# Output projection in rounded halves, two low parts on GpSimd, all orders set anew with nine streams

## The chip, the cores and the metric

One core of a Trainium2 chip runs the whole program in one launch. The metric is the device time of that launch in microseconds; every time here is of this one core. The engines are TensorE (PE in the rows, PEld for its weight loads), VectorE (DVE), ScalarE (ACT), GpSimd (POOL) and SyncE (SP), which issues the DMAs.

## The reference

`x` is 128 graphs of 128 nodes with 256 features, in float32. Four residual layers follow each other, each fed with `h = relu(layernorm(x))`:

```python
h = relu(layernorm(x)); x = x + L0(h)   # 8 heads of 32, masked by adj
#   qkv = h @ w_qkv; attn = softmax(where(adj == 0, -inf, q k^T * scale)); o = attn v
#   o = o @ w_proj + b_proj; L0 = o + layernorm(o) * gamma + beta
h = relu(layernorm(x)); x = x + L1(h)   # rel = adj^T * (h Wq^T)(h Wk^T)^T; rel / ||rel||; rel @ (h Wv^T)
h = relu(layernorm(x)); x = x + L2(h)   # hw = h W; e = leaky_relu(s1 + s2) * adj; elu(softmax(e) hw + beta hw)
h = relu(layernorm(x)); x = x + L3(h)   # (adj h) @ weight + bias
```

## The kernel before

The 128 graphs are 64 pairs, and one pair goes through the four layers in a software pipeline of `STREAMS = 8` stages. Step `t` of the unrolled loop works on eight pairs at once: stage `s` of it on pair `p_s = t - s`, if `on[s]`. Each engine has its own `step`, a list of blocks written out by hand in the order in which that engine is to take them; nothing else orders the work. An engine waits at a semaphore when a block needs what another engine makes (`wait_ge(..., done(p))`), when it would overwrite a single buffer that is still to be read (`wait_before`: the reader of the pair before must be through), or when a PSUM bank is still held by its last readers (`bank_free`). The eight PSUM banks (`mid[:, 0..3]` and `bank4..7`) are shared by some twenty uses, by a table of names at the top.

What the text below speaks of, in the order of the data:

- `z[k]` is the normalised input of layer `k`. PE transposes it (L329) into PSUM; ACT writes its relu, rounded to fp32r, as `h_t[k][0]` (the high part, L581, L589 and L644), and DVE writes the rest, relu minus high part, as `h_t[k][1]` (the low part, `relu_lo`, L730). A product of two such pairs is three fp32r matmuls (`product`, L313: high by high, high by low, low by high).
- `h_t[0]` feeds three products: q and k in the step in which it is made (stage 0) and the values v0 in the next step (stage 1). It is a single buffer, so ACT may write the next pair's high part only when v0 of the pair before is through (`v0_psum`).
- `scores()` (L357) fills the four banks of `mid`; DVE masks them and takes the least value of each row (`least_masked(r)`, L715); ACT takes the exponentials of head group `r` (`exps(r)`, L541, four activations); PE transposes them (`transpose_probs(r)`, L348); ACT copies each bank to SBUF; PE multiplies by the values and by ones (`heads_times_values`, L369 and L373). Scores and heads run on small tiles of the array (32 rows or 32 columns), all else on the whole array.
- ACT makes the reciprocal of the sums (L655, L658), DVE the scaled heads `o_t` (L830), and PE the output projection in plain float32 (`rows_f32`, L320).
- Layer 1 multiplies `h_t[1]` by the folded `w_qk` (g, then `g_t` copied by ACT, L563) and by `w_v` (v1), layer 2 `h_t[2]` by `w_gat` (hw, with `e_sum` made by ACT from it, L638), layer 3 `y_t` by `w_out`.
- POOL takes the inverse square roots (L903, L905, L914) and four elementwise products or sums (L927, L934, L938, L942).

Of the kernel before, what the change touches and what calls it, by code (L numbers as in the profile page):

```python
# [6 lines left out]
def gnn_stack(nc, x, adj, adj_t, w_qkv, w_proj, b_proj, gamma, beta_ln, w_q, w_k, w_v_t,  # L7
# [21 lines left out]
    STREAMS = 8  # L29
# [5 lines left out]
    with ctx:  # L35
# [27 lines left out]
        w_qk_p = parts("w_qk", [128, C, D])  # L63
        w_gat_p = parts("w_gat", [128, C, DX])
# [50 lines left out]
        o_t = sb("o_t", [128, 2, C, N])  # L115
        o = sb("o", [128, 2, D])
# [33 lines left out]
        q_bank = bank6[:]  # L150
        k_bank = mid[:, 1]
        v_bank = bank6[:]
        p0_bank = bank5[:]
        p1_bank = mid[:, 3]
        p2_bank = bank4[:]
        p3_bank = bank7[:]
        heads_bank = bank5[:]
        sums_bank = bank7[:]
        o_bank = bank5[:]
        z1_bank = bank6[:]  # L160
        g_bank = bank4[:]
        v1_bank = bank7[:]
        rel_bank = mid[:, 3]
        rel_v_bank = mid[:, 2]
        z2_bank = mid[:, 2]
        hw0_bank = mid[:, 2]
        hw1_bank = mid[:, 1]
        s2_bank = mid[:, 0]
        att_bank = mid[:, 0]
        u_bank = mid[:, 0]  # L170
        y_t_bank = bank4[:]
        y_bank = bank7[:]
# [13 lines left out]
        y_lo_ready = sem("y_lo_ready")  # L186
        shift0_ready = sem("shift0_ready")
# [64 lines left out]
        SPLIT = [(w_v_sb[:], w_v_p)]  # L252
# [26 lines left out]
        def _(sp):  # L279
# [9 lines left out]
            def step(t, par, load, store):  # L289
                pb, p_out = t - 1, t - 7  # L290

                if load:
                    i = (par + 1) % 2
                    sp.wait_ge(z_ready[0], done(pb))
                    sp.wait_ge(xb_ready, done(pb))
                    sp.dma_start(x0[:, i], x_pairs[pb + 2]).then_inc(x_in[i], 16)
                if store:
                    i = (par + 7) % 2
                    sp.wait_ge(x4_ready, done(p_out))
                    sp.dma_start(out_pairs[p_out], x4[:, i]).then_inc(x_out[i], 16)  # L300

            for t in range(PAIRS + 7):
                step(t, t % 2, 1 <= t < PAIRS + 1 - 2, t >= 7)
# [4 lines left out]
        def _(pe):  # L308
# [91 lines left out]
            def step(t, par, on):  # L400
                p0, p1, p2, p3, p4, p5, p6, p7, p8 = [t - s for s in range(STREAMS + 1)]

                if on[1]:
                    pe.wait_ge(q_ready, done(p1))
                    pe.wait_ge(k_ready, done(p1))
                    bank_free(pe, (e_sum_ready, p5, 2), (x3_ready, p6, 1), (att_t_ready, p6, 1))
                    bank_free(pe, (k_ready, p1, 1), (hw_ready, p5, 2))
                    bank_free(pe, (x2_ready, p4, 2), (hw_ready, p5, 2), (h_lo_ready[2], p5, 1))
                    bank_free(pe, (probs_t_ready[1], p2, 1), (sum_sq_ready, p4, 1))
                    scores().then_inc(scores_psum, 1)  # L410
                    pe.wait_ge(h_lo_ready[0], done(p1))
                    bank_free(pe, (h1_full_ready, p3, 1), (q_ready, p1, 1), (h_lo_ready[0], p1, 1))
                    rows(halves(v_bank), h_t[0], w_qkv_p, 2 * D, D).then_inc(v0_psum, 1)
                if on[3]:
                    pe.wait_ge(h_lo_ready[1], done(p3))
                    bank_free(pe, (y_lo_ready, p7, 1), (probs_t_ready[2], p2, 1))
                    columns(g_bank, w_qk_p, 0, h_t[1]).then_inc(g_psum, 1)
                if on[7]:
                    pe.wait_ge(y_lo_ready, done(p7))
                    bank_free(pe, (ln_sum_ready, p2, 1), (probs_t_ready[3], p2, 1), (v1_ready, p4, 1))  # L420
                    rows(halves(y_bank), y_t_p, w_out_p, 0, D).then_inc(y_psum, 1)
                if on[2]:
                    pe.wait_ge(o_norm_ready, done(p2))
                    bank_free(pe, (o_norm_ready, p2, 1), (probs_t_ready[0], p2, 1))
                    rows_f32(halves(o_bank), lambda b, c: o_t[:, b, c], w_proj_sb).then_inc(o_psum, 1)
                if on[0]:
                    pe.wait_ge(z_ready[0], done(p0))
                    bank_free(pe, (v0_ready, p1, 1), (h1_full_ready, p3, 1), (q_ready, p1, 1))
                    transposes(z0_bank, z[0]).then_inc(h_t_psum[0], 1)
                if on[4]:  # L430
                    pe.wait_ge(z_ready[2], done(p4))
                    bank_free(pe, (max_ready[2], p1, 1), (x2_ready, p4, 2), (hw_ready, p5, 2))
                    transposes(z2_bank, z[2]).then_inc(h_t_psum[2], 1)
                if on[3]:
                    pe.wait_ge(g_ready, done(p3))
                    pe.wait_ge(h1_full_ready, done(p3))
                    bank_free(pe, (max_ready[3], p1, 1), (probs_t_ready[1], p2, 1))
# [5 lines left out]
                if on[5]:  # L443
                    pe.wait_ge(att_norm_ready, done(p5, 2))
                    bank_free(pe, (max_ready[0], p1, 1), (e_sum_ready, p5, 2), (x3_ready, p6, 1))
                    for b in range(2):
                        last = pe.transpose(att_bank[:, b * N:(b + 1) * N], att_norm[:, b], ident[:])
                    last.then_inc(att_t_psum, 1)
                if on[1]:
                    pe.wait_ge(probs_ready[2], done(p1))  # L450
                    bank_free(pe, (g_ready, p3, 1), (y_lo_ready, p7, 1))
                    transpose_probs(2).then_inc(probs_t_psum[2], 1)
                if on[3]:
                    pe.wait_ge(h_lo_ready[1], done(p3))
                    bank_free(pe, (x4_ready, p7, 1), (ln_sum_ready, p2, 1), (probs_t_ready[3], p2, 1))
                    rows(halves(v1_bank), h_t[1], w_v_p, 0, D).then_inc(v1_psum, 1)
                if on[5]:
                    pe.wait_ge(att_t_ready, done(p5))
                    bank_free(pe, (att_t_ready, p5, 1), (max_ready[0], p1, 1), (e_sum_ready, p5, 2))
                    for b in range(2):  # L460
                        last = pe.matmul(u_bank[:, b * D:(b + 1) * D], att_t[:, b], hw[:, b, 0:D], start=True, stop=True)  # L461
                    last.then_inc(u_psum, 1)
                if on[1]:
                    pe.wait_ge(probs_ready[0], done(p1))
                    bank_free(pe, (o_ready, p2, 1), (o_norm_ready, p2, 1))
                    transpose_probs(0).then_inc(probs_t_psum[0], 1)
                if on[3]:
                    pe.wait_ge(rel_sq_ready, done(p3))
                    for b in range(2):
                        last = pe.matmul(rel_bank[:, 256 + b:257 + b], rel_sq[:, b], ones[:, 0:1], start=True, stop=True)  # L470
                    last.then_inc(sum_sq_psum, 1)
                if on[4]:
                    pe.wait_ge(h_lo_ready[2], done(p4))
                    bank_free(pe, (h_lo_ready[2], p4, 1), (max_ready[2], p1, 1), (x2_ready, p4, 2))
# [511 lines left out]
```

## Time and profile before

| | |
|---|---|
| time, median of 3 runs | 1482.62 us (1481.49 to 1482.86) |
| profiled execution: time, span | 1483.83 us, 1482.0 us |
| PE busy, share of the span | 1448.4 us, 98% |
| DVE, ACT, POOL busy | 1296.7, 1169.9, 606.9 us |
| mean granted TensorE clock | 0.991 of full speed |

The profiled execution's time lies 1.8 us above its span and 1.2 us above the median. A share of the span is an average over a start, an even middle and an end, which are read apart.

### The profile page before, as it was taken

The page shows a single profiled execution, that of the slowest core. Times are in us where ns is not written, and L with a number is a line of the kernel's source. Part 1 is how long each engine was busy: PE and PEld are TensorE (multiplying, and loading weights), DVE is VectorE, ACT ScalarE, POOL GpSimd, SP SyncE. Part 2 cuts the span into 40 slices and gives each one's busy share as a digit, 9 for nine tenths or more (in the row PEclk, how much of TensorE's full clock was granted, in tenths as well). Part 3 has the DMA queues.
Part 4 walks back from the last instruction along what each step waited for, and adds up shares of the span by engine and source line. Part 5 has one row for each costly group of instructions (what it writes and reads, how often), then busy time and mean ns, then how long its engine had stood idle before and what let it go on. Part 6 is the DMA issues. An engine that isn't in the chain of part 4 may idle for free.

```text
span 1482.0 us, 47177 instructions
## 1 busy us (share of the span) xinstructions
PE 1448.4 (98%) x15880; PEld 1375.0 (93%) x15880; DVE 1296.7 (87%) x5774; ACT 1169.9 (79%) x2948; POOL 606.9 (41%) x977
## 2 busy tenths in 40 slices
PE   6999999999999999999999999999999999999996
PEld 5899999999999999999999999999999999999985
DVE  3889988998989889889889889889889889889884
ACT  4788878878878878878878888888888878878763
POOL 3244434434434434444444444444444344344342
PEclk9999999999999999999999999999999999999997
DMA  3000101101000001000000010010010010000000
GB/s 111 16 16 23 30 17 30 30 18 30 24 23 30 22 25 30 19 28 30 17 31 30 16 31 30 16 31 30 17 30 30 16 30 30 17 30 30 11 21 30
DMA packets 38111, 39.87 MB, mean 27 GB/s; under 512 B 2416, under 2 KB 37488, under 8 KB 37872
## 3 DMA queue, kind: packets, MB, share of 16 engines
q1 hardware_dynamic: 37872, 36.84, 8.4%
q8 instruction: 131, 2.15, 0.6%
q14 instruction: 108, 0.88, 0.2%
HBM read 20.05 MB, written 16.78 MB: 25 GB/s over the span
## 4 chain that ended last, share of the span: by engine, by line
PE 95%; DVE 3%; issue 1%; POOL 0%; DMA 0%; ACT 0%; SPq 0%; POOLq 0%; DVEq 0%; ACTq 0%
PE bank L313 31%; PE mid L313 12%; PE bank L320 7%; PE bank L348 5%; PE mid L357 5%; PE bank L369 4%; PE mid L440 4%; PE mid L461 4%; PE bank L493 4%; PE bank L329 4%; PE bank L373 4%; PE mid L512 4%; PE mid L348 2%; PE mid L329 2%; PE mid L470 1%
## 5 line engine op out<-in xcount | busy, mean ns | idle before, releaser
L541 ACT ACTIVATE probs<-masked,neg_max 128x128 f32<-128x128 f32 x1024 | 312.0, 391 | 0.2 <-DVE neg_max L715 0.2
L715 DVE CUSTOM_DVE_ANT_0 masked<-mid,mask 128x128 f32<-128x128 f32 x1024 | 230.9, 287 | 18.1 <-issue 12.3
L905 POOL TENSOR_TENSOR rstd<-var_eps,minus_half 128x2 f32<-128x2 f32 x320 | 222.0, 694 | 25.1
L934 POOL TENSOR_TENSOR x3b<-x_up,b_out_less 128x512 f32<-128x512 f32 x64 | 82.3, 1287 | 283.1 <-DVE x L854 283.1
L903 POOL TENSOR_TENSOR var_eps<-mean_var,eps 128x2 f32<-128x2 f32 x320 | 62.9, 197 | 291.4 <-DVE mean_var L709 291.2
L705 DVE BATCH_NORM_STATS2 stats<-x 128x6 f32<-128x256 f32 x384 | 142.8, 413 | 3.5 <-DMA x<-in_x 3.5
L320 PE MATMUL bank<-w_proj_sb,o_t 128*128 128x256 f32 x512 | 121.0, 379 | 0.1
L348 PE MATMUL bank<-ident,probs 128*128 128x128 f32 x768 | 115.5, 273 | 1.9 <-ACT probs L541 1.0
L798 DVE SCALAR_TENSOR_TENSOR x<-mid,inv_norm,x 128x256 f32<-128x256 f32 x128 | 56.0, 480 | 70.1 <-PE mid L512 70.1
L914 POOL TENSOR_TENSOR inv_norm<-sum_sq,minus_half 128x2 f32<-128x2 f32 x64 | 66.7, 1043 | 119.8 <-DVE sum_sq L773 119.8
L938 POOL TENSOR_TENSOR xb<-x,b_proj_beta 128x512 f32<-128x512 f32 x64 | 81.5, 1273 | 60.7 <-DVE o_res L862 60.7
L369 PE MATMUL bank<-probs_t,v 128*32 128x128 f32 x2048 | 104.4, 276 | 0.0
L373 PE MATMUL bank<-probs_t,ones 128*32 128x128 f32 x2048 | 102.8, 273 | 0.0
L320 PEld LDWEIGHTS bank<-w_proj_sb,o_t 128*128 128x128 f32 x512 | 92.4, 190 | 10.3 <-DVE o_t L830 0.3
L348 PEld LDWEIGHTS bank<-ident,probs 128*128 128x128 f32 x768 | 91.7, 141 | 8.7 <-ACT probs L541 2.6
L621 ACT ACTIVATE probs_t<-bank 128x512 f32<-128x512 f32 x64 | 38.3, 598 | 74.6 <-PE bank L348 74.6
L724 DVE TENSOR_SCALAR z<-x,mean_var,rstd 128x256 f32<-128x256 f32 x256 | 92.1, 402 | 5.5 <-POOL rstd L905 5.3
L730 DVE SCALAR_TENSOR_TENSOR h_t_lo<-bank,h_t_hi 128x512 fp32r<-128x512 f32 x128 | 87.3, 682 | 4.8 <-ACT h_t_hi L589 4.3
L709 DVE BATCH_NORM_AGGREGATE mean_var<-stats 128x2 f32<-128x6 f32 x640 | 77.7, 163 | 13.8
L715 DVE DVE_READ_ACCUMULATOR2_ANT neg_max<- 128x1 f32 x1024 | 85.8, 84 | 0.0
L329 PE MATMUL bank<-ident,z 128*128 128x128 f32 x512 | 77.0, 273 | 2.9 <-issue 2.0
L313 PE MATMUL mid<-w_gat_hi,h_t_hi 128*128 128x258 f32 x256 | 79.0, 309 | 0.0
(142 smaller groups left out, 5373.4 us busy)
## 6 DMA issues: line engine op xcount, KB each, us to landing
x<-in_x SPq DMA_DIRECT2D x64, 256.0 KB, 2.9
out_x<-x SPq DMA_DIRECT2D x64, 256.0 KB, 3.2
w_qkv_sb<-in_w_qkv SPq DMA_DIRECT2D x1, 768.0 KB, 4.9
w_q_sb<-in_w_q SPq DMA_DIRECT2D x1, 256.0 KB, 4.8
w_k_sb<-in_w_k SPq DMA_DIRECT2D x1, 256.0 KB, 5.0
w_v_sb<-in_w_v_t SPq DMA_DIRECT2D x1, 256.0 KB, 5.7
w_proj_sb<-in_w_proj SPq DMA_DIRECT2D x1, 256.0 KB, 5.9
w_gat_x<-in_w_gat SPq DMA_DIRECT2D x1, 256.0 KB, 6.4
```

Of the source, the lines that this page charges most:

```text
L313: last = pe.matmul(dst, pick_l(lhs_t[a], c), pick_r(rhs[b], c), start=n == 0, stop=n == len(terms) - 1)
L320: last = pe.matmul(dsts[b], lhs_t(b, c), w[:, c], start=c == 0, stop=c == C - 1)
L329: last = pe.transpose(dst[:, (c * 2 + b) * N:(c * 2 + b + 1) * N], src[:, b, c * 128:(c + 1) * 128], ident[:])
L348: last = pe.transpose(dst[:, s * N:(s + 1) * N], probs[:, r, s], ident[:])
L369: pe.matmul(heads_bank[at, to], v0[:, b, hc * RG + r], probs_t[:, r, s], start=True, stop=True, tile_position=(0, r * HD))
L373: last = pe.matmul(sums_bank[at, to], ones[:], probs_t[:, r, s], start=True, stop=True, tile_position=(0, r * HD))
L541: last = act.activation(probs[:, r, s], masked[:, r, s], ACT.Exp, scale=-1.0, bias=neg_max[:, r, s:s + 1])
L705: dve.bn_stats(stats[:, k, b], src[:, b]).then_inc(ln_stats[k], 1)
L715: last = dve.tensor_tensor_reduce(out=masked[:, r, s], in0=mid[:, r, s * N:(s + 1) * N], in1=mask[:], scale=1.0, scalar=LARGE, op0=ALU.add ...
L724: last = dve.tensor_scalar(z[k][:, b], src[:, b], mean_var[:, k, b, 0:1], rstd[:, k, b:b + 1], ALU.subtract, ALU.mult)
L730: dve.scalar_tensor_tensor(h_t[k][1][:].rearrange("p c n -> p (c n)"), bank, 0.0, h_t[k][0][:].rearrange("p c n -> p (c n)").bitcast(f32), ...
L905: pool.tensor_tensor(rstd[:, k], var_eps[:, k], minus_half[:], ALU.pow).then_inc(ln_rstd[k], 1)
```

## The change

The input of the output projection is now split like the others: ACT rounds `o_t` to `o_t_p[0]`, POOL takes the rest as `o_t_p[1]`, and PE does twelve fp32r matmuls in place of four float32 ones; `w_proj` is split once at the start. The low part of `h_t[1]` is taken on POOL from `h_t1_full` in SBUF, no longer on DVE from PSUM, and `h_t1_full` no longer waits for the low part. The loop has nine stages: the last sum and the store of a pair are in stage 8, before in stage 7, and some blocks of layers 1 to 3 lie a step later. The blocks of every engine stand in a new order, and 21 uses of PSUM have other banks. ACT copies the folded weights in step 0, ahead of the first `z[0]`, before in step 1. The core of the diff, without the blocks that only stand elsewhere:

```diff
-    STREAMS = 8
+    STREAMS = 9
+        w_proj_p = parts("w_proj", [128, C, D])
+        o_t_p = parts("o_t", [128, 2, C, N])
...
-        q_bank = bank6[:]
-        k_bank = mid[:, 1]
-        v_bank = bank6[:]
+        q_bank = mid[:, 0]
+        k_bank = bank6[:]
+        v_bank = mid[:, 1]
         p0_bank = bank5[:]
...
-        g_bank = bank4[:]
+        g_bank = bank5[:]
...
-        SPLIT = [(w_v_sb[:], w_v_p)]
+        SPLIT = [(w_v_sb[:], w_v_p), (w_proj_sb[:], w_proj_p)]
...
-                    rows_f32(halves(o_bank), lambda b, c: o_t[:, b, c], w_proj_sb).then_inc(o_psum, 1)
+                    pe.wait_ge(o_lo_ready, done(p2))
+                    for b in range(2):
+                        last = product(o_bank[:, b * D:(b + 1) * D], o_t_p, w_proj_p,
+                                       lambda a, c: a[:, b, c], lambda a, c: a[:, c])
...
+                    act.wait_ge(o_norm_ready, done(p2))
+                    wait_before(act, o_psum, p2)
+                    act.activation(o_t_p[0][:], o_t[:], ACT.Copy).then_inc(o_hi_ready, 1)
...
-                    act.wait_ge(h_lo_ready[1], done(p3))
+                    act.wait_ge(h_t_psum[1], done(p3))
                     wait_before(act, rel_psum, p3)
                     act.activation(flat(h_t1_full), z1_bank, ACT.Relu).then_inc(h1_full_ready, 1)
...
-            run(act, step, [(1, copy_fold)])
+            run(act, step, [(0, copy_fold)])
...
-                    relu_lo(1, p3, z1_bank)
...
+                    pool.wait_ge(o_hi_ready, done(p2))
+                    pool.tensor_tensor(o_t_p[1][:], o_t[:], o_t_p[0][:].bitcast(f32), ALU.subtract).then_inc(o_lo_ready, 1)
...
+                    pool.wait_ge(h1_full_ready, done(p3))
+                    pool.wait_ge(h_hi_ready[1], done(p3))
+                    pool.tensor_tensor(flat(h_t[1][1]), flat(h_t1_full), flat(h_t[1][0]).bitcast(f32), ALU.subtract)\
+                        .then_inc(h_lo_ready[1], 1)
```

**First place: ACT, from the high part of `h_t[0]` to `g_t`.** Before, in one step of the even middle (the semaphores waited for stand in brackets; each row of `probs` is followed by three more of its kind, left out):

```order
L563 ACTIVATE g_t<-bank4 128x512 [waits rel_psum,g_psum]
L541 ACTIVATE probs<-masked,neg_max 128x128 [waits probs_t_psum2,max_ready2]
...
L541 ACTIVATE probs<-masked,neg_max 128x128 [waits probs_t_psum0,max_ready0]
...
L589 ACTIVATE h_t0_hi<-bank6 128x512 [waits v0_psum,h_t_psum0]
L541 ACTIVATE probs<-masked,neg_max 128x128 [waits probs_t_psum3,max_ready3]
...
L541 ACTIVATE probs<-masked,neg_max 128x128 [waits probs_t_psum1,max_ready1]
```

Of the change, across the border of two steps:

```order
L655 ACTIVATE h_t1_full<-bank7 128x512 [waits rel_psum,h_t_psum1]
L659 ACTIVATE h_t0_hi<-bank6 128x512 [waits v0_psum,h_t_psum0]
L548 ACTIVATE probs<-masked,neg_max 128x128 [waits probs_t_psum1,max_ready1]
...
L668 ACTIVATE e_sum<-bank5,hw 128x128 [waits e_leaky_ready,s2_psum]
...
L548 ACTIVATE probs<-masked,neg_max 128x128 [waits probs_t_psum3,max_ready3]
...
L548 ACTIVATE probs<-masked,neg_max 128x128 [waits probs_t_psum2,max_ready2]
...
L548 ACTIVATE probs<-masked,neg_max 128x128 [waits probs_t_psum0,max_ready0]
...
L566 ACTIVATE probs_t<-mid 128x512 [waits heads_psum,probs_t_psum1]
L569 ACTIVATE probs_t<-mid 128x512 [waits heads_psum,probs_t_psum3]
L573 ACTIVATE g_t<-bank5 128x512 [waits rel_psum,g_psum]
```

`g_t` stood ahead of the exponentials and now stands behind all sixteen of them and two copies, and the high part of `h_t[0]` stands directly ahead of them.

**Second place: PE, from the values v0 to the transposes of head group 0** (the first row of each product of twelve and of each group of four). Before:

```order
L313 MATMUL bank6<-w_qkv_hi,h_t0_hi 128x256 [waits h1_full_ready,h_lo_ready0]
...
L313 MATMUL bank4<-h_t1_hi,w_qk_hi 128x256 [waits y_lo_ready,h_lo_ready1]
...
L313 MATMUL bank7<-w_out_hi,y_t_hi 128x256 [waits ln_sum_ready,y_lo_ready]
...
L320 MATMUL bank5<-w_proj_sb,o_t 128x256 [waits o_norm_ready]
...
L329 MATMUL bank6<-ident,z0 128x128 [waits v0_ready,z_ready0]
```

Of the change:

```order
L332 MATMUL bank6<-ident,z0 128x128 [waits hw_ready,z_ready0]
...
L316 MATMUL mid<-w_qkv_hi,h_t0_hi 128x256 [waits max_ready1,h_lo_ready0]
...
L316 MATMUL bank7<-w_proj_hi,o_t_hi 128x256 [waits h1_full_ready,o_lo_ready]
...
L351 MATMUL mid<-ident,probs 128x128 [waits max_ready3,probs_ready1]
...
L316 MATMUL bank5<-h_t1_hi,w_qk_hi 128x256 [waits e_sum_ready,h_lo_ready1]
...
L351 MATMUL mid<-ident,probs 128x128 [waits max_ready2,probs_ready3]
...
L316 MATMUL bank4<-w_v_hi,h_t1_hi 128x256 [waits x2_ready,h_lo_ready1]
...
L316 MATMUL bank6<-h_t0_hi,w_qkv_hi 128x256 [waits h_lo_ready0]
...
L351 MATMUL bank5<-ident,probs 128x128 [waits g_ready,probs_ready0]
```

The transposes of `z0` now stand ahead of v0, and behind v0 there is one product (the output projection) ahead of the first transposes of exponentials; five groups further on stands a wait for `g_t`, whose bank head group 0 now shares.

**Third place: PE around the small tiles.** Before, the heads (L369, L373) and the scores (L357) stand side by side:

```order
L329 MATMUL bank6<-ident,z1 128x128 [waits q_ready,z_ready1]
...
L373 MATMUL bank7<-probs_t,ones 32x128 x4
L357 MATMUL mid<-k_t,q_t 128x128 [waits k_ready,x2_ready,e_sum_ready,probs_t_ready1,q_ready]
L357 MATMUL mid<-k_t,q_t 128x128 x15
L313 MATMUL bank6<-w_qkv_hi,h_t0_hi 128x256 [waits h1_full_ready,h_lo_ready0]
```

Of the change, a product of layer 2 and a small one of layer 1 stand between them:

```order
L418 MATMUL mid<-hw,att_t 128x256
...
L376 MATMUL mid<-probs_t,ones 32x128 x4
L316 MATMUL bank7<-w_gat_hi,h_t2_hi 128x258 [waits k_ready,h_lo_ready2]
...
L435 MATMUL bank5<-ones,rel_sq 128x1
L360 MATMUL mid<-k_t,q_t 128x128 [waits x3_ready,y_lo_ready,q_ready,ln_sum_ready,k_ready]
L360 MATMUL mid<-k_t,q_t 128x128 x15
L332 MATMUL bank7<-ident,z1 128x128 [waits hw_ready,z_ready1]
```

PE goes over to small tiles twice a step where it went once, and back twice.

## Rows read from the trace of the kernel before

**Rows 1.** The page, busy us (share of the span) xinstructions

```profile
PE 1448.4 (98%) x15880; PEld 1375.0 (93%) x15880; DVE 1296.7 (87%) x5774; ACT 1169.9 (79%) x2948; POOL 606.9 (41%) x977
```

**Rows 2.** Windows: stretch, length, busy of PE, PEld, DVE, ACT, POOL, clock, DMA

```profile
400.00:600.00 200.00, 200.00 (x2226) 190.60 (x2225) 180.49 (x803) 162.95 (x412) 84.46 (x135) 1.00 0.09 26
1420.00:1482.00 62.00, 45.75 (x280) 40.96 (x278) 37.12 (x112) 24.72 (x62) 19.58 (x30) 0.83 0.08 27
```

**Rows 3.** Timeline of PE: start, us, engine, line, work, number of records

```profile
601.79 1.89 PE L320 MATMUL bank<-w_proj_sb,o_t 128*128 128x256 f32 x8
603.52 0.60 PE L329 MATMUL bank<-ident,z 128*128 128x128 f32 x4
603.95 0.60 PE L329 MATMUL mid<-ident,z 128*128 128x128 f32 x4
...
624.12 1.89 PE L320 MATMUL bank<-w_proj_sb,o_t 128*128 128x256 f32 x8
```

**Rows 4.** Timeline of PE around heads and scores, and of the next product

```profile
616.26 0.60 PE L329 MATMUL bank<-ident,z 128*128 128x128 f32 x4
616.79 0.43 PE L369 MATMUL bank<-probs_t,v 128*32 128x128 f32 x8
...
618.34 0.40 PE L373 MATMUL bank<-probs_t,ones 128*32 128x128 f32 x8
618.67 1.17 PE L357 MATMUL mid<-k_t,q_t 32*128 32x128 f32 x32
619.78 0.39 PE L313 MATMUL bank<-w_qkv_hi,h_t_hi 128*128 128x256 f32 x1
620.00 0.28 PE L313 MATMUL bank<-w_qkv_lo,h_t_hi 128*128 128x256 f32 x1
...
621.31 0.28 PE L313 MATMUL bank<-h_t_hi,w_qk_hi 128*128 128x256 f32 x1
...
622.74 0.28 PE L313 MATMUL bank<-w_out_hi,y_t_hi 128*128 128x256 f32 x1
```

**Rows 5.** Timeline of PE at the end: heads with no scores behind them

```profile
1419.06 0.40 PE L373 MATMUL bank<-probs_t,ones 128*32 128x128 f32 x8
1419.40 0.39 PE L313 MATMUL bank<-h_t_hi,w_qk_hi 128*128 128x256 f32 x1
1419.62 0.27 PE L313 MATMUL bank<-h_t_lo,w_qk_hi 128*128 128x256 f32 x1
```

**Rows 6.** Timeline of ACT, [idle before and who ended it]

```profile
605.98 0.59 ACT L589 ACTIVATE h_t_hi<-bank 128x512 fp32r<-128x512 f32 x1
606.46 2.44 ACT L541 ACTIVATE probs<-masked,neg_max 128x128 f32<-128x128 f32 x8
...
615.60 0.63 ACT L638 ACTIVATE e_sum<-mid,hw 128x128 f32<-128x128 f32 x2
...
621.51 0.60 ACT L553 ACTIVATE v<-bank 128x512 f32<-128x512 f32 x1 [0.45 <-PE bank L313]
```

**Rows 7.** Timeline of ACT and PE at the start: transposes that wait for exponentials

```profile
23.19 2.44 ACT L541 ACTIVATE probs<-masked,neg_max 128x128 f32<-128x128 f32 x8
...
24.51 0.66 PE L348 MATMUL bank<-ident,probs 128*128 128x128 f32 x4 [0.49 <-ACT probs L541]
```

**Rows 8.** A group of POOL (us, mean ns, idle); one DVE line, ns min/median/max

```profile
L938 POOL TENSOR_TENSOR xb<-x,b_proj_beta 128x512 f32<-128x512 f32 x36 | 45.8, 1272 | 16.3 <-DVE o_res L862 16.3
...
L809 DVE SCALAR_TENSOR_TENSOR shift<-mean_var,rstd x64: 152/309/1234, 5.7 to 1377.5; 128x2 f32<-128x2 f32 x64
```

**Rows 9.** Timeline of PE: scores that open and close the even middle

```profile
127.34 1.17 PE L357 MATMUL mid<-k_t,q_t 32*128 32x128 f32 x32
...
1400.34 1.17 PE L357 MATMUL mid<-k_t,q_t 32*128 32x128 f32 x32
```

**Rows 10.** Timeline of ACT in the first 12 us

```profile
7.55 1.08 ACT L663 ACTIVATE z<-x,shift,rstd 128x256 f32<-128x256 f32 x2
...
11.80 0.59 ACT L537 ACTIVATE w_qk_hi<-bank 128x512 fp32r<-128x512 f32 x1
```

More of the change, by code:

```diff
@@ new lines, in step @@
+                if on[5]:
+                    pe.wait_ge(hw_ready, done(p5, 2))
+                    bank_free(pe, (sum_sq_ready, p4, 1), (probs_t_ready[0], p2, 1), (g_ready, p4, 1))
+                    for b in range(2):
+                        last = pe.transpose(s2_bank[:, b * N:(b + 1) * N], hw[:, b, D + 1:D + 2].to_broadcast([128, 128]),
+                                            ident[:])
+                    last.then_inc(s2_psum, 1)
+                if on[0]:
+                    pe.wait_ge(z_ready[0], done(p0))
+                    bank_free(pe, (hw_ready, p5, 2), (k_ready, p1, 1))
+                    transposes(z0_bank, z[0]).then_inc(h_t_psum[0], 1)
@@ L433, in step @@
                     transposes(z2_bank, z[2]).then_inc(h_t_psum[2], 1)
+                if on[0]:
+                    pe.wait_ge(h_lo_ready[0], done(p0))
+                    bank_free(pe, (max_ready[0], p1, 1))
+                    columns(q_bank, w_qkv_p, 0, h_t[0]).then_inc(q_psum, 1)
+                if on[5]:
+                    pe.wait_ge(att_norm_ready, done(p5, 2))
+                    bank_free(pe, (v1_ready, p3, 1), (x2_ready, p4, 2), (o_norm_ready, p2, 1))
+                    for b in range(2):
+                        last = pe.transpose(att_bank[:, b * N:(b + 1) * N], att_norm[:, b], ident[:])
+                    last.then_inc(att_t_psum, 1)
@@ L453, in step @@
[L453 to L471, printed above, removed]
@@ L518, in step @@
-                if on[1]:
-                    for r in range(RG):
-                        pe.wait_ge(probs_t_ready[r], done(p1))
-                    pe.wait_ge(v0_ready, done(p1))
-                    bank_free(pe, (probs_t_ready[0], p1, 1), (o_ready, p2, 1))
-                    bank_free(pe, (probs_t_ready[3], p1, 1), (v1_ready, p3, 1), (x4_ready, p7, 1))
-                    heads_times_values().then_inc(heads_psum, 1)
-            run(pe, step, [(0, fold), (2, next_weights), (4, last_weights)])
+            run(pe, step, [(0, fold), (2, next_weights), (5, last_weights)])
@@ L658, in step @@
                     act.activation(inv_sum[:], ln_sum[:], ACT.Exp, scale=-1.0).then_inc(inv_sum_ready, 1)
+                if on[5]:
+                    act.wait_ge(hw_psum, done(p5))
+                    wait_before(act, u_psum, p5)
+                    for b, bank in ((0, hw0_bank), (1, hw1_bank)):
+                        act.activation(hw[:, b], bank[:, 0:DX], ACT.Copy).then_inc(hw_ready, 1)
                 if on[0]:
```

576 lines of the change are left out of this document (288 added, 288 removed).

## The prediction

> **What bounds the kernel now.** I read the busy shares first: PE 98%, DVE 87%, ACT 79%, POOL 41% [rows 1]. Then stretches, since a share says nothing of waits. In the middle PE is busy 200.00 of 200 us at full clock, with DVE at 180.5, ACT at 163.0 and POOL at 84.5; in the last 62 us PE works 45.75 at a mean clock of 0.83 [rows 2]. So in the middle nothing but PE's own work sets the pace, and every other engine has idle time: 2.2 us a step on DVE, 4.1 on ACT. The step is read from two output projections in a row: 624.12 - 601.79 = 22.33 us [rows 3]. From the scores at 127.34 to those at 1400.34 lie 57 such steps: 1273.0 / 22.33 = 57.0 [rows 9]. What is left is a start of 127 and an end of 82 us.
>
> The trace is to be read by where the next group starts, not by durations, since matmuls overlap. The float32 output projection holds PE for 603.52 - 601.79 = 1.73 us, four transposes for 0.43 to 0.44 [rows 3], a product of twelve fp32r matmuls for 622.74 - 621.31 = 1.43 [rows 4].
>
> **The projection.** Twelve fp32r matmuls for four float32 ones: 1.73 becomes 1.43, so 0.30 us of PE a step are saved, 17 us over 57 steps. That is all that the change can win in the middle.
>
> **Small tiles, now twice.** Going over to them costs time. The four transposes ahead of the heads hold PE for 0.53 instead of 0.43, so entering costs 0.10. From the last heads to the scores it is 0.33, where such a group takes 0.22 (618.67 less 618.34; the eight groups from 616.79 take 1.88 with that gap), so changing from small to small costs 0.11 [rows 4]. Leaving is seen alone where no scores follow: 1419.40 - 1419.06 = 0.34 instead of 0.22, and then 0.22 to the second matmul instead of 0.12, so 0.22 [rows 5]. The scores leave alike (the same 0.22 behind 619.78) [rows 4]. Before, a step pays 0.10 + 0.11 + 0.22 = 0.43. Now it enters twice and leaves twice. The exit from the scores goes to transposes, which no row shows; its bounds are the 0.11 of small to small and the 0.22 of rows 5, and I take 0.20, near the exit. That makes 0.20 + 0.22 + 0.20 = 0.62, 0.19 more than before. The Trainium skill, TensorEngine Tiling (Array Packing), Key Properties, says that changing the tiling mode drains the engine; the rows agree, and the page gives no price. PE's own work thus comes to 22.33 - 0.30 + 0.19 = 22.22 us a step.
>
> **A wait that the new order makes.** On ACT the high part of `h_t[0]` needs v0 of the pair before to be through, because v0 reads the buffer that is overwritten. Before, v0 stood at the top of PE's step and the high part came in the middle of ACT's, long after. Now PE has v0, the projection, then the transposes of group 1, and ACT has the high part, then `exps(1)`. So: v0 ends, ACT writes the high part, ACT makes the exponentials, and only then can PE transpose them; PE has one product to do meanwhile. Call V the start of the matmul behind v0.
>
> ACT starts 0.20 after it: the copy of v0 starts at 621.51 [rows 6], and the next product had started at 621.31 [rows 4]. The high part holds ACT for 606.46 - 605.98 = 0.48. Each ACT row overlaps the next by about 0.10, so eight exponentials hold it for 2.34, four for 1.17, and the fourth ends 1.27 after the first began [rows 6]. To V + 1.95 comes 0.05 until PE starts: of the exponentials that begin at 23.19 the fourth ends at 24.46, and the transposes begin at 24.51; they take 0.66 instead of 0.60, so restarting costs 0.06 [rows 7]. PE is ready at V + 1.43 and starts at V + 2.00: **0.57 of waiting and 0.06 of restart.**
>
> ACT goes on without rest: from V + 1.85 `e_sum`, two in 0.63, 0.53 with the overlap off [rows 6], to V + 2.38; twelve exponentials, 3.51, to V + 5.89; two copies of 0.48 to V + 6.85; `g_t`, which takes 0.60 as the copy of v0 does [rows 6], ends at V + 7.45. PE's transposes of group 0 wait for it, since they now share its bank: V + 7.50. PE gets there from V + 2.00 by transposes 0.44 + 0.06, g 1.43 (its bank is freed by `e_sum`, done at V + 2.48 + 0.05, so 0.03 more), transposes 0.44, v1 1.43 and k 1.43, at V + 7.26. It waits 0.24, and restarts for 0.06. **Both together: 0.57 + 0.06 + 0.03 + 0.24 + 0.06 = 0.96 us a step.** Nothing hides it: PE is in order, so all behind the transposes is as late, v0 of the next step too, and the loop closes through it. A step lasts 22.22 + 0.96 = 23.18, 0.85 more than before, 57 x 0.85 = 48.5 us.
>
> **What lies beside other work.** ACT gains the rounding of `o_t`, 0.49: 16.3 + 1.8 = 18.1 us a step becomes 18.6 of 23.2. DVE loses one low part and stands at 19.5. POOL gains two sums of 512 columns of 1.27 us [rows 8] and goes from 9.4 to 12.0. The low part of `o_t`: from the end of the heads two activations (1.3), the scaling on DVE (0.7), two copies and `z` on ACT (1.6), the rounding (0.6), POOL (1.3), some 5.4 us with handovers; PE has hw, the small product, scores, transposes, two products and v0 to do, over 6.5. So its cover is about 1 us; if POOL is behind by one sum of 1.27 the projection is late, but up to 0.57 of that only takes the place of the wait above. The low part of `h_t[1]` comes some 2 us before g. SP's store moves by a step and nothing waits for it. Its load of the next `x` moves too: it waits for `xb` on POOL and is now issued in the very step that reads it, but `xb` is POOL's third block and the statistics stand in the middle of DVE's step, several us later; if that cover went, DVE would wait first, which has time to spare.
>
> **Start and end.** The folded weights are now copied ahead of the first `z`, so that ends at 12.4 + 1.1 = 13.5, not at 8.6 [rows 10]; PE had the fold to do until 11.3, so between 0 and 2.2 us are lost, and I take 1. The ACT wait of about 1 us also falls on three or so of the steps of the start: 4 in all. The end has one more step, in which PE mostly waits; it had 16.3 us of idle in the last 62 [rows 2]. Bounds 0 and 8; I take 4. Sum: 48.5 + 8 = 56.5 on the span of 1482.0, so 1538.5; on the median of 1482.62 it is 1539.
>
> **The rivals.** *(A) The forecast*, both waits bind: 1539, chance 0.70. With the exit from the scores at 0.11 or 0.22, 0.05 more or less of each handover, and start and end at 0 or 16, it lies between 1525 and 1554.
>
> *(B) Only the first wait binds*, because ACT's queue behind it runs faster than its rows: 22.22 + 0.63 = 22.85, 57 x 0.52 + 8 = 38 more, 1520. Against it: the exponentials of rows 6 are a run without a gap. Chance 0.07.
>
> *(C) DVE and POOL block each other.* A DVE operation of two values per partition takes 152 ns at the least, 309 in the median and 1234 at the most, as long as POOL's sum [rows 8]: it was held until POOL was through. The eight or so DVE operations a step that read two operands in SBUF would meet POOL's sums more often now, each up to 1.3 us. DVE has 23.2 - 19.5 = 3.7 us a step; only above that does the step grow. If half of them met a sum at its middle it would be 2.6, hidden; at twice that the step is 24.7 and the time 1482.6 + 57 x 2.37 + 8 = 1626. Chance 0.07, most of it for a spill of 0.3 to 0.6 us a step, 1539 + 57 x 0.3 or 0.6, 1556 to 1573. The Trainium skill, SBUF — State Buffer, Who interferes with whom, calls this an exclusive lock between a DVE instruction with two SBUF inputs and a GpSimd instruction that reads SBUF; by that rule the two new POOL sums count in full, and the trace agrees with it.
>
> *(D) No wait at all*, PE stays fed: 57 x -0.11 + 8 = +2, 1484. For it speaks only that before all of ACT's waits were hidden. Chance 0.08.
>
> *(E) The other side, faster.* The only mechanism is the projection's 0.30, if the second visit to small tiles is free and ACT's high part meets no held buffer: 57 x -0.30 = -17, with start and end at 0, 1466. It decides if less than 0.30 us a step is lost in waits and tile changes; rows 5 alone put 0.22 against it. Chance 0.08.
>
> **How the numbers follow.** About 3 us (0.2%) is what a measurement of this kernel tells from no change. The likeliest is A, 1539. A range of eight in ten takes A and B and the nearer part of C: 1517 to 1562. Faster is E, 0.08; within 0.2% most of D, 0.06; slower all else, 0.86.
>
> **What would show it.** In the changed kernel's trace: scores 23.2 us apart; one idle of 0.5 to 0.6 us a step on PE ahead of the transposes from `probs`, ended by ACT (about 33 us in all), and one of some 0.25 ahead of those into bank5; ACT idle for nearly 2 us ahead of the high part of `h_t[0]`, ended by PE's product v0; the projection at 1.43. I am wrong if scores lie 22.2 apart (D), if the first wait stands and the second does not (B), or if the idle on PE is ended by DVE or by the low part of `o_t` (C).

## The result: 1538.8 us, 3.8% slower

The changed kernel takes 1538.82 us (median of 4 runs, 1537.79 to 1540.17), the kernel before 1482.05 us beside it (4 runs, 1480.25 to 1482.86). The ratio is 1.0381, with a 95% interval of 1.0368 to 1.0393. The forecast was 1539, from two waits that the new order makes. The total came out; the terms inside it did less well, and the experiments below take them one at a time.

The page of the changed kernel, busy us (share of the span) xinstructions, and the shares of the chain that ended last:

```profile
PE 1465.2 (95%) x16136; PEld 1370.3 (89%) x16136; DVE 1311.9 (85%) x5710; ACT 1178.4 (77%) x3012; POOL 763.8 (50%) x1107
PE 86%; ACT 6%; issue 4%; DVE 2%; POOL 1%; DMA 0%; ACTq 0%; SPq 0%; DVEq 0%; POOLq 0%
```

The span has grown from 1482.0 to 1536.1 us, PE's busy time by 17 us only, and its share has fallen from 98% to 95% [rows 1]. So PE waits. Two windows of the changed kernel (columns as in [rows 2]), the middle and the last 62 us:

```profile
400.00:600.00 200.00, 195.89 (x2207) 183.59 (x2206) 176.96 (x770) 157.74 (x402) 101.02 (x148) 1.00 0.09 26
1474.00:1536.00 62.00, 42.81 (x290) 38.54 (x287) 40.45 (x116) 25.15 (x64) 24.57 (x36) 0.87 0.08 27
```

Where PE was busy for 200.00 of 200 us it is now busy for 195.89, at the same full clock, while DVE and ACT are less busy than before [rows 2]. No engine is a new bound; PE and ACT wait for each other. The timeline of PE shows how long the even middle is, by its first and last scores (start, us, engine, line, work, records; as [rows 9]):

```profile
133.48 1.17 PE L360 MATMUL mid<-k_t,q_t 32*128 32x128 f32 x32
...
1452.95 1.17 PE L360 MATMUL mid<-k_t,q_t 32*128 32x128 f32 x32
```

Between them lie 57 steps: 1319.47 / 57 = 23.15 us, where a step was 22.33. That is 57 x 0.815 = 46.5 us. The start has grown by 133.48 - 127.34 = 6.1 us [rows 9], the end from 81.7 to 83.1, by 1.5. The sum, 54.1, is the growth of the span.

The timeline of ACT in one step of the changed kernel, with the idle time before a row and who ended it in brackets:

```profile
902.15 0.60 ACT L659 ACTIVATE h_t_hi<-bank 128x512 fp32r<-128x512 f32 x1 [1.91 <-PE mid L316]
902.64 1.27 ACT L548 ACTIVATE probs<-masked,neg_max 128x128 f32<-128x128 f32 x4
903.81 0.61 ACT L668 ACTIVATE e_sum<-bank,hw 128x128 f32<-128x128 f32 x2
904.31 3.62 ACT L548 ACTIVATE probs<-masked,neg_max 128x128 f32<-128x128 f32 x12
...
908.78 0.59 ACT L573 ACTIVATE g_t<-bank 128x512 f32<-128x512 f32 x1
```

And PE in the same step (the first row is the last matmul of v0, the second the first of the output projection, which stands directly behind it):

```profile
901.77 0.28 PE L316 MATMUL mid<-w_qkv_hi,h_t_lo 128*128 128x256 f32 x1
901.89 0.28 PE L316 MATMUL bank<-w_proj_hi,o_t_hi 128*128 128x256 f32 x1
...
903.97 0.66 PE L351 MATMUL mid<-ident,probs 128*128 128x128 f32 x4 [0.50 <-ACT probs L548]
904.57 0.36 PE L316 MATMUL bank<-h_t_hi,w_qk_hi 128*128 128x256 f32 x1
...
906.07 0.60 PE L351 MATMUL mid<-ident,probs 128*128 128x128 f32 x4
906.43 0.36 PE L316 MATMUL bank<-w_v_hi,h_t_hi 128*128 128x256 f32 x1
...
909.52 0.63 PE L351 MATMUL bank<-ident,probs 128*128 128x128 f32 x4
```

Read them side by side. The last matmul of v0 gives way to the projection at 901.89 and ends at 901.77 + 0.28 = 902.05. ACT has stood idle for 1.91 us behind that wait, and writes the high part at 902.15. Its fourth exponential ends at 902.64 + 1.27 = 903.91, and PE's transposes start at 903.97. Two more places are late without a bracket, since the bracket shows only the idle time that a modelled end leaves. The product g starts 0.60 us after the transposes, where the next group of this kind gives way after 0.36 (906.07 to 906.43), behind `e_sum`, which ends at 904.42. The transposes at 909.52 start behind `g_t`, which ends at 909.37. The waits of the changed kernel between 300 and 1200 us (in total, times, longest) say the same of 39 steps: ACT waits for PE's v0, and PE waits for ACT's exponentials. The second row is a wait of DVE, which has time to spare; it only shows that `e_sum` is late for others too:

```profile
ACT h_t_hi L659 <- PE mid L316: 74.3, 39, 1.9
DVE e_leaky L753 <- ACT e_sum L668: 61.6, 39, 1.6
...
PE mid L351 <- ACT probs L548: 19.5, 39, 0.5
```

### The profile page after: what moved, and what is told of

Same layout as the page of the kernel before. It is cut to its first block, busy times and chain, and to the rows that moved or that the text cites. A ratio compares the mean times of both kernels' runs of the same rounds, so it can differ in the third digit from the quotient of the medians.

```text
span 1536.1 us, 47950 instructions
## 1 busy us (share of the span) xinstructions
PE 1465.2 (95%) x16136; PEld 1370.3 (89%) x16136; DVE 1311.9 (85%) x5710; ACT 1178.4 (77%) x3012; POOL 763.8 (50%) x1107
## 4 chain that ended last, share of the span: by engine, by line
PE 86%; ACT 6%; issue 4%; DVE 2%; POOL 1%; DMA 0%; ACTq 0%; SPq 0%; DVEq 0%; POOLq 0%
PE bank L316 25%; PE mid L316 17%; PE mid L351 6%; PE bank L332 6%; ACT probs L548 5%; PE mid L360 4%; PE bank L372 4%; PE mid L411 4%; PE bank L529 4%; PE mid L376 4%; PE mid L418 4%; PE bank L454 3%; PE bank L351 3%; PE bank L435 1%; PE bank L521 1%
## 5 line engine op out<-in xcount | busy, mean ns | idle before, releaser
L351 PE MATMUL mid<-ident,probs 128*128 128x128 f32 x768 | 119.8, 279 | 33.9 <-ACT probs L548 33.9
L659 ACT ACTIVATE h_t_hi<-bank 128x512 fp32r<-128x512 f32 x64 | 38.4, 600 | 121.1 <-PE mid L316 120.3
L351 PEld LDWEIGHTS mid<-ident,probs 128*128 128x128 f32 x768 | 87.0, 141 | 47.3 <-ACT probs L548 47.2
L332 PE MATMUL bank<-ident,z 128*128 128x128 f32 x768 | 118.7, 277 | 6.5 <-DVE z L732 3.3
L805 DVE SCALAR_TENSOR_TENSOR x<-o_gam,rstd,o_res 128x256 f32<-128x256 f32 x128 | 116.7, 954 | 1.0 <-POOL rstd L910 1.0
L950 POOL TENSOR_TENSOR o_t_lo<-o_t,o_t_hi 128x512 fp32r<-128x512 f32 x64 | 81.7, 1276 | 69.1 <-ACT o_t_hi L647 69.0
L919 POOL TENSOR_TENSOR e_mask<-e_leaky,adj_sb 128x256 f32<-128x256 f32 x64 | 47.0, 735 | 129.9 <-DVE e_leaky L753 129.8
L753 DVE SCALAR_TENSOR_TENSOR e_leaky<-e_sum 128x256 f32<-128x256 f32 x64 | 27.9, 436 | 93.4 <-ACT e_sum L668 93.4
L376 PE MATMUL mid<-probs_t,ones 128*32 128x128 f32 x2048 | 102.8, 273 | 0.0
L332 PEld LDWEIGHTS bank<-ident,z 128*128 128x128 f32 x768 | 85.9, 141 | 15.4 <-DVE z L732 4.2
```

The source lines that it names most:

```text
L332: last = pe.transpose(dst[:, (c * 2 + b) * N:(c * 2 + b + 1) * N], src[:, b, c * 128:(c + 1) * 128], ident[:])
L351: last = pe.transpose(dst[:, s * N:(s + 1) * N], probs[:, r, s], ident[:])
L376: last = pe.matmul(sums_bank[at, to], ones[:], probs_t[:, r, s], start=True, stop=True, tile_position=(0, r * HD))
L805: dve.scalar_tensor_tensor(x1[:, i3, b], o_gam[:, b], rstd[:, LN_O, b:b + 1], o_res[:, b], ALU.mult, ALU.add).then_inc(x1_ready, 1)
```

## The experiments

Nine kernels. All but two start from the changed kernel; "projection alone" and "late split" start from the kernel before. The step is the median distance between scores of the trace. All medians are in us, and the kernel before took 1482.75, 1482.53 and 1482.36 in the three comparisons.

| experiment | median | ratio, 95% interval | step |
|---|---|---|---|
| the change | 1538.82 | 1.0381 [1.0368, 1.0393] | 23.147 |
| `h_t[0]` twice | 1469.94 | 0.9915 [0.9900, 0.9930] | 22.047 |
| `exps(1)` first | 1471.07 | 0.9919 [0.9902, 0.9935] | 22.047 |
| `g_t` early | 1528.87 | 1.0311 [1.0296, 1.0327] | 22.947 |
| both moves | 1471.67 | 0.9928 [0.9912, 0.9945] | 22.047 |
| `exps(3)` ahead of `exps(1)` | 1647.88 | 1.1112 [1.1096, 1.1129] | 24.434 |
| more work on POOL | 1542.21 | 1.0403 [1.0388, 1.0419] | 23.146 |
| projection alone | 1470.95 | 0.9921 [0.9905, 0.9938] | 22.013 |
| projection alone, late split | 1469.18 | 0.9919 [0.9905, 0.9933] | 22.013 |
| `h_t[0]` twice, late split | 1471.49 | 0.9926 [0.9912, 0.9939] | 22.047 |

### `h_t[0]` twice: the reason for the wait is taken away

The theory is that ACT waits for v0 only because it would overwrite its input. With a second buffer nothing is held, and no block moves:

```diff
+        h_t0 = [h_t[0], parts("h_t0b", [128, C, 2 * N])]
...
-                    wait_before(act, v0_psum, p0)
-                    act.activation(flat(h_t[0][0]), z0_bank, ACT.Relu).then_inc(h_hi_ready[0], 1)
+                    wait_two_before(act, v0_psum, p0)
+                    act.activation(flat(h_t0[p0 % 2][0]), z0_bank, ACT.Relu).then_inc(h_hi_ready[0], 1)
```

> The changed kernel with one edit: h_t[0] has two buffers, taken in turn, so that ACT's high part of the next pair no longer waits for the product v0 that reads the old one. Theory (ACT is held by that buffer and PE then waits behind ACT): the 0.65 us idle of PE ahead of the transposes of group 1 goes, ACT's work starts 1.9 us earlier, so the waits for e_sum and g_t behind it go too; a step falls from 23.15 to PE's own work of 22.1, 57 x 1.05 = 60 us and some 4 at the start: 1474, below the kernel before. Rival (DVE and POOL blocking each other sets the step): the buffer changes nothing, 1539. Rival (small tiles and the start cost it): 1530 to 1539.

It took 1469.94 us: 69 less than the changed kernel, and less than the kernel before. The step is 22.047, 1.10 shorter. A window of it shows PE fed again, as [rows 2] did; DVE at 185 and POOL at 108 of 200 do not hold it:

```profile
400.00:600.00 200.00, 200.00 (x2284) 192.15 (x2284) 185.18 (x806) 167.51 (x430) 107.82 (x155) 1.00 0.08 26
```

On ACT the wait of 1.91 us is one of 0.42, for the transposes of `z0` and no longer for v0:

```profile
902.88 0.60 ACT L660 ACTIVATE h_t_hi<-bank 128x512 fp32r<-128x512 f32 x1 [0.42 <-PE bank L333]
903.38 1.27 ACT L549 ACTIVATE probs<-masked,neg_max 128x128 f32<-128x128 f32 x4
```

The other two waits went as well, though nothing was done about them: the product g starts 0.35 us after the transposes (905.52 to 905.87) and not 0.60, and no idle time stands ahead of group 0. `e_sum` and `g_t` were late only because ACT had been held before them.

### `exps(1)` first: the order alone

The buffer stays single, but ACT makes the first exponentials before it turns to the high part, so that PE's transposes no longer hang on v0 by way of ACT:

```diff
-                if on[0]:
-                    act.wait_ge(h_t_psum[0], done(p0))
-                    wait_before(act, v0_psum, p0)
-                    act.activation(flat(h_t[0][0]), z0_bank, ACT.Relu).then_inc(h_hi_ready[0], 1)
                 if on[1]:
                     ...
                     exps(1).then_inc(probs_ready[1], 1)
+                if on[0]:
+                    act.wait_ge(h_t_psum[0], done(p0))
+                    wait_before(act, v0_psum, p0)
+                    act.activation(flat(h_t[0][0]), z0_bank, ACT.Relu).then_inc(h_hi_ready[0], 1)
```

> The changed kernel with one block of ACT moved: the exponentials of group 1 stand ahead of the high part of h_t[0], not behind it; the buffer stays single, ACT still waits for v0 there. Theory: PE finds its exponentials ready while ACT waits; ACT's chain to g_t is 1.2 us shorter from v0 on, 6.3 against PE's 6.6, so no wait is left: 1474 as with the second buffer. If the held buffer itself and not its place ahead of the exponentials is what costs: 1530 or more. DVE and POOL blocking: 1539.

1471.07 us, with the same step of 22.047. So the price was neither the buffer nor the order by itself, but the two together: a block with a held output directly ahead of the block that PE needs next. ACT still stands idle for v0, 0.75 us a step in the mean from 400 to 1200 us, and that costs nothing. Either repair gives all of it back.

### `g_t` early: the second wait alone

```diff
+                if on[4]:
+                    act.wait_ge(g_psum, done(p4))
+                    wait_before(act, rel_psum, p4)
+                    act.activation(flat(g_t), g_bank, ACT.Copy).then_inc(g_ready, 1)
                 if on[2]:
                     act.wait_ge(max_ready[0], done(p2))
                     wait_before(act, probs_t_psum[0], p2)
                     exps(0).then_inc(probs_ready[0], 1)
```

(the same block is taken out behind the two copies of `probs_t`).

> The changed kernel with one block of ACT moved: the copy g_t stands ahead of the exponentials of group 0 and the copies of groups 1 and 3, not behind them. Theory of two waits: only the second goes (0.17 us and 0.03 of restart a step), the first and the one for e_sum stay: 57 x 0.2 = 11 us less, 1527. If the second wait only passes on what the first made: 1539. If the second sets the loop alone: 1480.

1528.87 us, step 22.947: 0.20 less than the changed kernel. In the middle that is 11.5 us; the end gives 3 of them back (86.2 us behind the last scores, for 83.1), for a reason that stays open. So the second wait costs 0.20 a step with its restart and can be removed by itself, while the first stays: PE's timeline in this kernel still has it. The product g starts 0.60 us behind these transposes, so the wait for `e_sum` stays as well.

```profile
919.56 0.66 PE L351 MATMUL mid<-ident,probs 128*128 128x128 f32 x4 [0.50 <-ACT probs L548]
```

### Both moves at once

The two edits above together: if the second wait were an independent cost, it would show here again.

> The changed kernel with both moves on ACT: exponentials of group 1 ahead of the held buffer, g_t ahead of the exponentials of group 0. Theory: once the first is moved PE has no wait left to remove, so this is 1474 like the first move alone, within 2 us. If a wait for g_t or e_sum outlived the first move: lower than that by up to 57 x 0.2 = 11 us.

1471.67, step 22.047, as with the first move alone. The 0.20 is worth nothing once the first wait is gone.

### `exps(3)` ahead of `exps(1)`: the same wait made longer

This turns the mechanism the other way. PE wants group 1 first; ACT now makes group 3 ahead of it, and `e_sum` in between:

```diff
-                    act.wait_ge(max_ready[1], done(p1))
-                    wait_before(act, probs_t_psum[1], p1)
-                    exps(1).then_inc(probs_ready[1], 1)
+                    act.wait_ge(max_ready[3], done(p1))
+                    wait_before(act, probs_t_psum[3], p1)
+                    exps(3).then_inc(probs_ready[3], 1)
```

> The changed kernel with ACT's exponentials of group 3 ahead of those of group 1, behind the held buffer (e_sum between the two); nothing is added or left out, and PE's order stays. It lengthens the suspected chain from v0 to the transposes of group 1 by 1.17 + 0.53 us. Theory: those transposes start at V + 3.7 in place of V + 2.07, which eats the later waits of 0.4, so a step grows by about 1.3 us: 57 x 1.3 = 74, 1613. Rivals (DVE and POOL, small tiles): the same work in another order, 1539.

1647.88 us, 35 more than I had expected. PE's wait grew as it should, from 0.50 to 2.17 us, and most steps are 24.43, 1.29 longer than in the changed kernel. That alone is 73 us. But every third or fourth step is 26.0. In such a step, on PE's timeline, this happened:

```profile
600.07 0.28 PE L316 MATMUL bank<-h_t_hi,w_qk_lo 128*128 128x256 f32 x1
600.19 0.29 PE L316 MATMUL bank<-h_t_hi,w_qk_hi 128*128 128x256 f32 x1
...
600.69 0.41 PE L316 MATMUL bank<-h_t_hi,w_qk_hi 128*128 128x256 f32 x1
600.90 0.41 PE L316 MATMUL bank<-h_t_lo,w_qk_hi 128*128 128x256 f32 x1
...
603.84 0.28 PE L316 MATMUL bank<-w_v_hi,h_t_lo 128*128 128x256 f32 x1
603.97 0.28 PE L316 MATMUL bank<-w_v_hi,h_t_hi 128*128 128x256 f32 x1
```

The same matmuls follow each other every 0.12 us, then every 0.21, then every 0.12 again. Windows of this kernel give the granted clock (the third column from the end): 1.00 in the 35 us before, 0.55 in the stretch itself, while PE was busy all through it:

```profile
565.00:600.00 35.00, 30.66 (x344) 29.09 (x343) 29.25 (x146) 26.81 (x71) 17.19 (x25) 1.00 0.05 17
600.00:603.40 3.40, 3.40 (x20) 3.40 (x19) 3.36 (x13) 2.74 (x9) 2.49 (x4) 0.55 0.19 63
```

The records of the clock hold nothing but 1.00 and 0.50, that is 2.4 and 1.2 GHz, and 0.50 comes back throughout the middle. So the 57 steps take 24.932 us in the mean: (24.932 - 24.434) x 57 = 28 us of clock beside the 73 of waiting, and the start and the end are 11 longer. Together that is the 112.6 us by which its span, 1648.7, is above that of the changed kernel. The wait's own price was right; the fall of the clock, which came with it in this kernel alone, was not in my sum.

### More work on POOL: does the neighbour matter?

The rival that lost says that POOL's sums block DVE. Two more sums of 512 columns from SBUF, used by nothing, were added to each step of the changed kernel:

```diff
+                    pool.tensor_tensor(spare[:], both(b_proj_beta), both(b_out_less), ALU.add).then_inc(spare_ready, 1)
```

> The changed kernel with two more sums of 512 columns on POOL in every step (into a buffer that nobody reads; both inputs in SBUF), 2.55 us more of POOL, as much as the change added, one behind x3b and one ahead of the power for layer 1. Theory (ACT's order sets the step): hidden, 1539 to 1545, the step stays at 23.15. Rival (POOL's two new sums block DVE and that costs the time): as much again as the change lost, 1590.

1542.21 us, 3.4 more; the step is the same, 23.146, so the middle has none of it. The end has: 87.5 us behind the last scores, for 83.1. Whether the sums did that isn't shown, since `g_t` early has an end of 86.2 without them. POOL is busy for 126 of 200 us instead of 101, and DVE for 178.8 instead of 177.0: its spare time is still wide enough.

### The projection alone

All orders, banks and the eight streams of the kernel before, and only the projection split: ACT rounds ahead of the copy of v0, POOL subtracts ahead of `x3b`.

```diff
-                    rows_f32(halves(o_bank), lambda b, c: o_t[:, b, c], w_proj_sb).then_inc(o_psum, 1)
+                    for b in range(2):
+                        last = product(o_bank[:, b * D:(b + 1) * D], o_t_p, w_proj_p,
+                                       lambda a, c: a[:, b, c], lambda a, c: a[:, c])
+                    last.then_inc(o_psum, 1)
```

> The kernel before with its own orders and banks and eight stages, and only the split projection: w_proj split at the start, o_t rounded on ACT (ahead of the copy of v0), its low part on POOL (ahead of x3b), twelve fp32r matmuls. Theory (the loss is the new orders', the split is a gain): a step is 22.33 - 0.30 = 22.03, 57 x 0.30 = 17 us less, up to 3 us lost at the start where PE waits for the split w_proj: 1468. Rival (the split itself costs, by a late low part or by POOL blocking DVE): 1482 or more.

1470.95 us. The step is 22.013, so the projection saves 0.32. On PE the projection gives way after 1.41 us (624.24 to 625.65), where it was 1.73. The middle gives 18.2 us, and the start takes 7.2 of them back: pair 6's scores stand at 134.49, not at 127.34 [rows 9]. The end is 2.1 shorter.

### The projection alone, with `w_proj` split later

What the start lost could be POOL's splitting of `w_proj`, which stood ahead of the second pair's inverse square root, or the new chain by way of POOL. This kernel takes the first away: the split is done in step 2, where POOL is free.

```diff
             def last_constants():
+                split(*SPLIT[1], 3)
                 pool.wait_ge(late_const_in, 16 * len(LATE_CONSTS))
```

> The kernel before with the projection alone in rounded halves, and now w_proj split on GpSimd in step 2, ahead of the late weights, and no longer in step 1 ahead of the second pair's inverse square root. If the 7 us that the projection alone lost at the start come from that root (its first operation stood at 17.33 us there and at 15.66 in the kernel before), then the start is shorter again: the scores of pair 6 near 129, the step still 22.01, the time 1465 or 1466. The rival: the start is lost to the projection's own chain (heads, scaling, ACT, GpSimd) in steps where PE has no other work, and then the time stays at 1471.

Both were right in part. The scores of pair 6 stand at 131.99: 2.5 of the 7.2 us came back. The other 4.7 are still there, and PE's waits over the whole execution of this kernel name the chain (in total, times, longest):

```profile
PE bank L316 <- POOL o_t_lo L945: 5.9, 6, 2.1
```

Five of the six, 4.6 us, fall in the steps of the start and one in the end, where PE has little else to do and the chain ACT, POOL, PE lies open. In the middle it is covered. The median, 1469.18, has an interval that overlaps that of the kernel without the late split (0.9905 to 0.9933 beside 0.9905 to 0.9938), so the 2 us are read from the traces and not from the times.

### `h_t[0]` twice, with `w_proj` split later

> The changed kernel with h_t[0] in two buffers, and w_proj split behind w_v's two operations, each weight by itself. The first products wait for nothing of it in either case: 1470 as with two buffers alone, within 2 us, step 22.05.

1471.49, with pair 6's scores at 127.92 as without (127.93): nothing to win there. The fastest kernels are thus the six at 1469 to 1472, which the measurement does not tell apart. All keep the projection's halves and feed PE through the middle.

## Why the prediction held, and where it did not

**The mechanism** was the one forecast: the held buffer, ACT behind it, PE behind ACT, and the loop closing through v0. Taking away either half of it takes away all of the loss, and making it longer makes the loss longer.

**The first wait** was put at 0.57 + 0.06. From the projection's start to the transposes lie 903.97 - 901.89 = 2.08 us. Where no wait follows, the product holds PE for 1.41 (904.11 to 905.52 with `h_t[0]` twice), which leaves 0.67. Over the whole execution PE has 33.9 us of idle time of this kind, forecast about 33. ACT began 0.26 after the product behind v0 and not 0.20, and the restart is 0.06, as forecast (0.66 instead of 0.60).

**The wait for `e_sum`** was put at 0.03 and is 0.60 - 0.36 - 0.06 = 0.18. With `exps(3)` first, where `e_sum` is made earlier, the product follows the same restart after 0.41 (598.99 to 599.40), so the rest is indeed the wait. `e_sum` itself was on time: it ends 904.42 - 902.64 = 1.78 us after the first exponential, for a forecast of 1.80. It is the handover that was mis-sized. The product's matmul starts 0.15 after the end of `e_sum`, and I had carried the 0.05 of [rows 7] over from transposes that wait for exponentials. `g_t` shows 0.15 again (909.37 to 909.52). Why these handovers are longer than that one stays open.

**The second wait**, 0.24 + 0.06 in the forecast, costs 0.20 by experiment. With PE 0.2 us later at group 0, through the two waits before it, less was left to wait for.

Together the waits cost 23.147 - 22.047 = 1.10 a step, forecast 0.96; the three pieces, 0.67 + 0.06, 0.18 and 0.20, come to 1.11.

**The projection** saves 22.333 - 22.013 = 0.32, forecast 0.30: it holds PE for 1.41 and not for the 1.43 of the products in [rows 4].

**The tile changes** were the worst of the terms: +0.19 forecast. The kernel with the old orders and that with the new ones, both without waits and both with the split projection, differ by 22.047 - 22.013 = 0.03. The failed step is "Now it enters twice and leaves twice", with the same price for each. Three rows of PE's timeline in the changed kernel show what one of the entrances costs:

```profile
920.07 0.50 PE L435 MATMUL bank<-ones,rel_sq 128*128 128x1 f32 x4
920.50 1.17 PE L360 MATMUL mid<-k_t,q_t 32*128 32x128 f32 x32
921.61 0.66 PE L332 MATMUL bank<-ident,z 128*128 128x128 f32 x4
```

The scores follow the small product after 0.43 us. In the kernel before, the small product gave way to an fp32r product on the whole array:

```profile
608.66 0.50 PE L470 MATMUL mid<-ones,rel_sq 128*128 128x1 f32 x4
609.02 0.37 PE L313 MATMUL mid<-w_gat_hi,h_t_hi 128*128 128x258 f32 x1
609.23 0.28 PE L313 MATMUL mid<-w_gat_lo,h_t_hi 128*128 128x258 f32 x1
```

That is 0.36 us to the product and 0.21, not 0.12, from there to its second matmul: 0.45 without any change of tiles. So this entrance, behind matmuls of one column, costs nothing over what stood there before. The entrance to the heads costs its 0.10 in the changed kernel too, now behind matmuls of 256 columns: 915.67 to 916.63 is 0.96, where four such gave way to transposes after 0.86 (607.36 to 608.22). The exit from the scores to transposes takes the 0.11 of small to small, if the scores leave as the heads do, and 0.06 more (921.61 to 922.10 is 0.49, for 0.43 in [rows 3]), 0.17 where I took 0.20. By these rows the tiles cost 0.10 + 0.22 + 0 + 0.17 = 0.49, 0.06 more than before; what makes it 0.03 on the step is not known, since the new orders have other neighbours throughout. The Trainium skill, TensorEngine Tiling (Array Packing), Key Properties, says that a change of the tiling mode drains the engine, and gives no price; the rows with a price agree. Why one entrance costs 0.10 us and the other nothing no run here shows.

With 0.32 and 0.03 in the sum PE's own work is 22.05, where I had 22.22. That error of 0.17 and the error of 0.14 in the waits, of the other sign, nearly cancel: the step was forecast at 23.18 and is 23.15. The total was right to 1 us partly by that luck, and partly by another: the span grew by 54.1 us, where 56.5 was forecast, but the profiled execution of the kernel before lay 1.2 us above its median and that of the changed kernel 1.0 below.

**Start and end** were put at 4 and 4, and are 6.1 and 1.5, 7.6 in the place of 8. With `h_t[0]` twice, pair 6's scores stand at 127.93, so 5.5 of the 6.1 were the wait, which already bound in the steps of the start; I had counted it three times there. The first `z` ends at 13.5 as forecast (ACT in the changed kernel):

```profile
12.46 1.08 ACT L641 ACTIVATE z<-x,shift,rstd 128x256 f32<-128x256 f32 x2
```

**The rivals.** B, only the first wait, is excluded by `g_t` early: it costs 0.20. D, no wait, by the 0.50 us on PE. C was forecast to make DVE late by POOL's two new sums. There is blocking in the trace of the changed kernel. Two rows between 300 and 1200 us, one of DVE and one of POOL (us, mean ns, idle):

```profile
L805 DVE SCALAR_TENSOR_TENSOR x<-o_gam,rstd,o_res 128x256 f32<-128x256 f32 x78 | 74.2, 994 | 0.0
...
L933 POOL TENSOR_TENSOR x3b<-x_up,b_out_less 128x512 f32<-128x512 f32 x39 | 56.9, 1458 | 103.0 <-DVE x L799 103.0
```

The same DVE operation took 482 ns in the kernel before, and that sum 1288. They stand on each other: in the step above DVE's two start at 912.62 and last 1.90 us together, and POOL's sum starts at 912.78 and ends at 914.24. That is 1.0 us a step on DVE, which was put at 19.5 us a step and has 20.5 (176.96 of 200), and over 2 to spare. It comes from the new orders and an old sum, not from the two new ones. This operation, which has two inputs in SBUF, takes 475 ns at the least and 1514 at the most, and the second of the two in this step ends 0.28 us after POOL's sum. The Trainium skill, SBUF — State Buffer, Who interferes with whom, calls the ports that the two engines share an exclusive lock; the trace agrees. The new sums cost nothing in the middle, and two further ones none either. The low part of `o_t` kept its cover: it ends at 900.62, the projection starts at 901.89, 1.3 us later (forecast about 1). E, faster, was the wrong sign for this kernel and the right one for its parts: 1466 was its price, and the repaired kernels come to 1470 to 1472.

So the expected gain was there. The change wins 0.32 us a step by the projection, pays 0.03 for its new orders, and 1.10 for one place in ACT's order that a second buffer or a swap of two blocks repairs. Apart from that place the new orders are near neutral: `h_t[0]` twice against the projection alone has a start 6.6 us shorter, a middle 1.9 longer and an end 3.1 longer.

## What to carry to other kernels

When PE is busy for 200 of 200 us, a new order has little to win, and it can lose by a wait: for each block of an in-order engine whose output buffer is single, find the reader that must be through, and see what stands behind the block and who needs that. A second buffer for the one held operand was worth 69 us here, while the projection's own arithmetic was worth 18 in the middle and 12 in the time. Of several waits in one loop mend the earliest first; the later ones were its echoes, and taking the last one away by itself gave 0.20 of 1.10. Price a handover by a row of the same kind: 0.05 us from exponentials to transposes, and 0.15 from a sum or a copy to what waits for its bank.

## What the hardware did that I had not expected

The granted clock did not stay at one level in the kernel with the longer wait. With waits of 0.50 us a step in the bracket, PE busy for 195.9 of 200 us, it was 1.00 throughout the middle. With one wait of 2.17 us a step, PE busy for 182 of 200, it fell again and again to half, for 28 us of added time in all; the two windows of 200 us from 400 to 800 have 0.98 and 0.97. The Trainium skill, TensorE: Matmul & The Clock Gate, Part 1, says that the clock is set by how busy the engine has been lately. That agrees in direction. The drop shown above came while PE was working, 1.3 us after the wait in that step had ended (598.99). Where between the two kernels it begins no run here shows.

And the entrance to the scores' small tiles behind the one-column product cost nothing that can be seen, where the entrance to the heads' costs 0.10 us, before [rows 4] and in the changed kernel.
